# Attention tiles of 64 queries by 128 keys in place of 128 by 256

## What is computed

```python
x = x + layernorm(attention(layernorm(x)))
x = x + layernorm(ffn(layernorm(x)))

# attention: Q, K, V = x @ W.T + b, split into 16 heads
scores = Q @ K.T / sqrt(32) - (i - j)     # keys j <= query i; others -inf
out = softmax(scores) @ V                 # then @ Wo.T + bo
# ffn: x @ Hadamard, rounded per row to 4 bits, times a ternary weight
```

## Time and profile before

| | us |
|---|---|
| median of 3 runs | 1519.39 (1518.03 to 1520.32) |
| the profiled execution | 1518.89 |
| its span | 1517.2 |
| TensorE busy | 1410.3 (93%) |
| VectorE busy | 1110.3 (73%) |
| ScalarE busy | 744.7 (49%) |
| GpSimd busy | 566.5 (37%) |
| DMA queue of SP, share of 16 engines | 23.8% |

### The profile page before, as it was taken

The page is one execution under the profiler, slowest core; times in us unless marked ns, Lnnn a source line. Parts: engine busy times, 40 slices in busy tenths (PEclk is TensorE's granted clock), DMA queues, the critical chain, the costliest instruction groups (busy, mean ns, idle before and its releaser), DMA issues.

```text
span 1517.2 us, 39677 instructions
## 1 busy us (share of the span) xinstructions
PE 1410.3 (93%) x16320; PEld 954.9 (63%) x16320; DVE 1110.3 (73%) x2737; ACT 744.7 (49%) x1587; POOL 566.5 (37%) x618
## 2 busy tenths in 40 slices
PE   3789999999999999999999999999999999999852
PEld 2556666677656666666666766666666766666521
DVE  4667777777877777787777777877777787776662
ACT  3245554545545555555555545455454555554521
POOL 1132443333344443343444333344433334443321
PEclk9899999999999999999999999999999999999985
DMA  7322333222233322122333212233322222322010
GB/s 221 80 65 54 86 85 85 71 60 69 58 84 85 85 76 65 58 77 66 85 85 85 63 59 79 57 85 86 85 71 64 64 60 82 86 71 72 20 37 16
DMA packets 62073, 111.69 MB, mean 74 GB/s; under 512 B 13344, under 2 KB 14112, under 8 KB 61792
## 3 DMA queue, kind: packets, MB, share of 16 engines
q1 hardware_dynamic: 57200, 92.06, 23.8%
q0 software_dynamic: 4688, 17.04, 3.0%
HBM read 41.43 MB, written 16.78 MB: 38 GB/s over the span
## 4 chain that ended last, share of the span: by engine, by line
PE 73%; DVE 15%; ACT 4%; issue 3%; POOL 3%; DMA 1%; POOLq 0%; SPq 0%; DVEq 0%; ACTq 0%
PE f_job L977 38%; PE f_o L1100 10%; PE f_st L1081 6%; PE f_job L1131 4%; PE f_job L1149 3%; PE f_job L1006 2%; PE f_job L1123 2%; PE f_job L1049 2%; PE f_job L1061 2%; ACT f_y L505 2%; POOL f_z L377 2%; DVE f_bst L751 1%; DVE f_small L800 1%; ACT f_xTh L444 1%; PE f_job L1139 1%
## 5 line engine op out<-in xcount | busy, mean ns | idle before, releaser
L479 ACT ACTIVATE f_PT<-f_st 128x512 f32<-128x512 f32 (+1 forms) x512 | 262.9, 569 | 117.0 <-PE f_st L1081 117.0
L356 POOL TENSOR_SCALAR_AFFINE_SELECT f_PT<-f_PT 128x1024 f32<-128x1024 f32 x128 | 142.6, 1114 | 352.9 <-ACT f_PT L479 352.9
L705 DVE SCALAR_TENSOR_TENSOR f_stage<-f_job,f_bias,f_stage 128x256 f16<-128x256 f32 x256 | 112.0, 479 | 182.1 <-ACT f_stage L457 182.1
L350 POOL TENSOR_TENSOR f_small<-f_small,f_minus_half 128x2 f32<-128x2 f32 x128 | 98.3, 768 | 371.8 <-DVE f_small L684 285.8
L457 ACT ACTIVATE f_stage<-f_job,f_bias 128x256 f16<-128x256 f32 x256 | 107.5, 471 | 187.9 <-PE f_job L977 187.9
L1100 PE MATMUL f_o<-f_PT,f_V 128*32 128x128 f32 (+1 forms) x2816 | 172.3, 316 | 1.7 <-POOL f_PT L356 1.7
L1100 PE MATMUL f_o<-f_PT,f_ones 128*32 128x128 f32 (+1 forms) x2816 | 169.1, 312 | 0.0
L1081 PE MATMUL f_st<-f_stacks 128*128 128x128 f16 (+1 forms) x1408 | 150.1, 240 | 5.0 <-ACT f_PT L479 3.6
L977 PE MATMUL f_job<-f_xTh,f_wqh 128*128 128x256 f16 x512 | 140.5, 274 | 11.7 <-DVE f_wkl L603 5.9
L362 POOL TENSOR_TENSOR f_OTl<-f_o,f_OTh 128x256 f16<-128x256 f32 x128 | 84.7, 672 | 174.4 <-ACT f_OTh L493 174.4
L1081 PEld LDWEIGHTS f_st<-f_stacks 128*128 128x128 f16 x1408 | 116.5, 98 | 50.7 <-issue 7.1
(11 more groups left out here) (145 smaller groups left out, 3260.7 us busy)
## 6 DMA issues: line engine op xcount, KB each, us to landing
f_stacks<-f_stage SPq DMA_DIRECT2D x384, 128.0 KB, 2.4
f_xin<-x SPq DMA_DIRECT2D x32, 512.0 KB, 4.8
f_xres<-x SPq DMA_DIRECT2D x32, 512.0 KB, 4.1
out<-f_z POOLq DMA_DIRECT2D x32, 512.0 KB, 3.3
f_stacks<-rows_const SPq DMA_DIRECT2D x3, 512.0 KB, 5.7
f_stacks<-wqT SPq DMA_DIRECT2D x1, 1024.0 KB, 7.8
f_stacks<-wkT SPq DMA_DIRECT2D x1, 1024.0 KB, 10.5
f_stacks<-wvT SPq DMA_DIRECT2D x1, 1024.0 KB, 10.8
```

Of the source, the lines that this page charges most:

```text
L350: nc.gpsimd.tensor_tensor(dst, src, minus_half[:], ALU.pow).then_inc(done, 1)
L356: nc.gpsimd.affine_select(out=d, in_=d, compare_op=ALU.is_ge, fill=0.0, base=0, pattern=[[0, 4], [0, 2], [1, P]], channel_multiplier=-1).t ...
L479: nc.scalar.activation(PT[g % 2][:, r, lo:D], ps_st[r % 2][:, lo:D], ACT.Exp, scale=1.0 / SS).then_inc(expd, 1)
L705: nc.vector.scalar_tensor_tensor(stage[:, 2 * m + 1, g, :], bank("qk", g)[:, m * W2:(m + 1) * W2], bias[:, m, g:g + 1], stage[:, 2 * m, g, ...
```

## The change

Attention is cut by 64 queries. A tile of 64 queries now takes 128 keys: the 64 at its own place and the 64 before it. The chunks of 64 keys alternate between the upper and lower half of the partitions, so that each tile of queries has one chunk in each half and needs one product for its values. An odd chunk's two key chunks are one tile of `V`; an even chunk's lie in two tiles, so `Vmix` holds the lower half of V's tile beside the upper half of the tile before. It is filled by three on-chip DMAs a step (`mix_values`), issued by SyncE behind `restack`.

- `keys`: 5 products of 64 keys for each head (4 in the first step of a sequence) in place of 3 of 128, with 256 result columns in place of 512. Two heads share a PSUM bank and one semaphore increment.
- `exps`: one activation over two heads in place of two. In the first step of a sequence, two smaller ones.
- `clear_future`: two affine selects of half the columns, the first of them on 64 partitions.
- `weigh`: for each head four value products of 64 columns and one sum product of 256, with no accumulation; it waits for `v_mixed`, not `v_kept`.
- `V` has two buffers in place of three, `Vmix` has three, `PT` is half as large.

```diff
-        def parts(s):
-            return ([(s, 0, 0, P, 2 * P)] + ([(s - 1, 1, 0, 0, P)] if s % PER else [])
-                    + [(s, 1, 1, 3 * P, P)])
+        def keys_of(s):
+            last = [(1, s - 1, 3, 0, 1)] if s % PER else []
+            return [(0, s, 0, 0, 2)] + last + [(1, s, 1, 1, 2), (0, s, 2, 2, 2), (1, s, 3, 3, 1)]
+
+        def values_of(s, chunk):
+            keys = slice(0, P if chunk or s % PER else SUB)
+            return keys, (V[s % 2] if chunk % 2 else Vmix[s % 3])[keys, chunk // 2]
...
+            def mix_values(n):
+                sp.wait_ge(v_kept, TP * n + TP)
+                until(sp, pv_done, 4 * (n - 1))
+                lower, upper = slice(0, SUB), slice(SUB, P)
+                sp.dma_start(Vmix[n % 3][lower], V[n % 2][lower]).then_inc(v_mixed, 16)
+                sp.dma_start(Vmix[n % 3][upper, 1], V[n % 2][upper, 0]).then_inc(v_mixed, 16)
+                sp.dma_start(Vmix[(n + 1) % 3][upper, 0], V[n % 2][upper, 1]).then_inc(v_mixed, 16)
...
                 if has(s + 1):
                     restack(s + 1)
+                    mix_values(s + 1)
...
             def clear_future(s, g):
-                pool.wait_ge(expd, NH * s + 4 * g + 4)
-                d = PT[g % 2][:].rearrange("p r (a c) -> p r a c", c=P)[:, :, 1::2, :]
-                nc.gpsimd.affine_select(out=d, in_=d, compare_op=ALU.is_ge, fill=0.0, base=0,
-                                        pattern=[[0, 4], [0, 2], [1, P]],
-                                        channel_multiplier=-1).then_inc(masked, 1)
+                pool.wait_ge(expd, 2 * (4 * s + g) + 2)
+                tiles = PT[g % 2][:].rearrange("p r (t c) -> p r t c", c=P)
+                for odd in range(2):
+                    d = tiles[0:P if odd else SUB, :, :, odd * SUB:(odd + 1) * SUB]
+                    nc.gpsimd.affine_select(out=d, in_=d, compare_op=ALU.is_ge, fill=0.0, base=odd * SUB,
+                                            pattern=[[0, 4], [0, TP], [1, SUB]],
+                                            channel_multiplier=-1).then_inc(masked, 1)
...
             def keep_v(n, t):
...
                 until(act, pv_done, 4 * (n - 1))
+                until(act, v_mixed, (n - 1) * (16 * 3))
...
             def exps(s, g, half):
...
+                act.wait_ge(keyed, 2 * (4 * s + g) + half + 1)
+                until(act, pv_done, 4 * s + g - 1)
+                dst, src = PT[g % 2][:, 2 * half:2 * half + 2, :], ps_st[half][:].rearrange("p (r n) -> p r n", r=2)
+                if s % PER:
+                    nc.scalar.activation(dst, src, ACT.Exp, scale=1.0 / SS).then_inc(expd, 1)
...
             def keys(s, g, half):
...
+                until(pe, expd, 2 * (4 * s + g) + half - 1)
+                for i in range(2):
+                    h = 4 * (2 * half + i) + g
+                    for upper, js, c, q, w in keys_of(s):
+                        mm = pe.matmul(ps_st[half][upper * SUB:(upper + 1) * SUB,
+                                                   i * W2 + q * SUB:i * W2 + (q + w) * SUB],
+                                       Ks[js % 3][:, h, c * SUB:(c + 1) * SUB],
+                                       Qs[s % 3][:, h, q * SUB:(q + w) * SUB], start=True, stop=True)
+                mm.then_inc(keyed, 1)
...
             def weigh(s, g):
-                pe.wait_ge(masked, 4 * s + g + 1)
+                pe.wait_ge(masked, 2 * (4 * s + g) + 2)
...
-                    pe.wait_ge(v_kept, TP * s + TP)
+                    pe.wait_ge(v_mixed, (s + 1) * (16 * 3))
...
+                for c in range(W2 // SUB):
+                    keys, v = values_of(s, c)
+                    for r in range(4):
+                        rows = slice(r * HD, (r + 1) * HD)
+                        pe.matmul(dst[rows, c * SUB:(c + 1) * SUB], v[:, g * P + r * HD:g * P + (r + 1) * HD],
+                                  weights[keys, r, c * SUB:(c + 1) * SUB], start=True, stop=True)
+                for lo, hi in ((0, W2),) if s % PER else ((0, SUB), (SUB, W2)):
+                    keys, _ = values_of(s, lo // SUB)
+                    for r in range(4):
+                        mm = pe.matmul(dst[r * HD:(r + 1) * HD, W2 + lo:W2 + hi], ones[keys], weights[keys, r, lo:hi],
+                                       start=True, stop=True)
                 mm.then_inc(pv_done, 1)
```

41 lines of the change are left out of this document (11 added, 30 removed).

## The result

| | before | after |
|---|---|---|
| median (us) | 1519.14 (4 runs) | 1605.13 (1604.62 to 1605.91, 4 runs) |
| the profiled execution | 1518.89 | 1605.35 |
| its span | 1517.2 | 1603.5 |
| steps in the middle of the run | 43.5 to 44.1 | 46.0 to 47.9 |

The changed kernel takes 1.0566 times as long (95% interval 1.0548 to 1.0585): 86 us slower, where 30 us faster was forecast. A step is 47.0 us on average in place of 43.9. The time is outside the range and on the other side of zero.

The account below looks back on a forecast made before the run. VectorE's chain up to turn_x2 was taken to be as long as TensorE's work. Savings of 1.0 us in 24 steps with prior keys and 0.7 in 8 without made 30 us, so 1489 us, range 1460 to 1520.

Parts of the forecast that it names:

- What bounds the kernel: Up to turn_x2, VectorE's chain is as long as TensorE's work, so TensorE savings come through only as that chain shortens.
- weigh with prior keys: One weigh call on TensorE falls from 1.88 us to 1.05, saving 0.83 for each of four.
- keys amid full-width work: A keys call among full-width TensorE products costs 0.43 us against 0.44, change-over included; counted as no gain.
- rival 3: Loads of narrow weights on TensorE don't hide: weigh 1.44 us, keys 0.65, total 1513 us; chance 0.10.
- Transfers: Three more DMAs a step for values and mixing, 512 KB together, block nobody: cost 0, at most 5 us once per step.
- Behind T0: After T0, the start of turn_x2 (L1123), a step with prior keys gets 0.7 us shorter, from weigh's 0.83.
- VectorE's 1.19 idle: In steps with prior keys, VectorE's 1.19 us wait for ScalarE's inverse of weigh(s,0) goes away.
- From the end of `z_columns` to T0: Stretch of VectorE's chain before turn_x2: 11.10 us with a 0.61 wait for GpSimd's power and a 0.9 stall behind a select.
- the 25.5 us of the earlier trace: TensorE's wait at turn_x2 for VectorE's x2_norm, 9 times over the run, read as eight steps without prior and one more.
- VectorE's chain up to T0: VectorE's work before turn_x2 gets 0.3 us shorter a step; bounds 0.2 worse with both select stalls, 1.6 better with none.
- rival 4: GpSimd's selects stall VectorE longer, deciding from a pair of 1.6 us on; at 2.2 us the total is 1557; chance 0.13.
- Rival 1: VectorE's chain takes over as the bound: 1489 us, the forecast itself, own range 1470 to 1514; chance 0.70.

Follow-up runs that it names:

- e16: Changed kernel, own 64 keys always in the upper partitions, one select on 128 partitions, 16 products a keys call in place of 10: 1530.98 us, ratio 1.0081.
- e6: Changed kernel with the three transfers of mix_values left out from the fourth step on: 1603.94 us, ratio 1.0565.
- e3: Changed kernel with 12 products of 512 columns, results unread, put on TensorE ahead of turn_x2(k,0): 1547.11 us, ratio 1.0193.
- e4: Kernel before with each select of 1024 columns split in two of 512, both on 128 partitions: 1515.99 us, ratio 0.9985.
- e13: Changed kernel with the two selects in the other order, the 128-partition one first: 1604.15 us, ratio 1.0558.
- e15: Changed kernel with both selects on 128 partitions in the 24 steps with prior keys: 1542.66 us, ratio 1.0158.
- e1: Changed kernel with VectorE's square of qscale (L848) moved from behind scale_out to behind level(k-1,1): 1515.6 us, ratio 0.9982.
- e5: Kernel before with weigh cut to 512 columns, leaving out the previous tile's keys: 1527.35 us, ratio 1.0065.
- e8: e1 with weigh(s,2) moved ahead of turn_x2(k,0) in TensorE's order: 1466.86 us, ratio 0.9666.
- e2: Changed kernel with one select of 1024 columns on 128 partitions for the pair in the 24 steps with prior keys: 1535.51 us, ratio 1.0119.
- e12: e8 with keys(s,3,1) moved ahead of turn_x2(k,0) as well: 1470.0 us, ratio 0.9686.
- e9: e1 with 7 products of 512 columns without use ahead of turn_x2(k,0): 1496.7 us, ratio 0.9861.
- e11: Kernel before with the square of qscale placed later, behind the first bn_stats of z: 1518.67 us, ratio 1.0002.

## Why the prediction was wrong

**Right, and borne out.** What bounds the kernel: TensorE does wait for VectorE at `turn_x2` in nearly every step, 31 times. weigh with prior keys: 1.05 forecast, 1.01 measured. keys amid full-width work: 0.43 forecast; 0.36 to the start of the next plus 0.10 on the products behind (the 12 of `out_product` take 2.69 in place of 2.59 us) is 0.46, so indeed no gain there. Narrow loads hide (rival 3 falls, also with 16 of them in e16). Transfers: 0 (e6). Behind T0: 0.7 forecast, 0.79 in e3. VectorE's 1.19 idle is gone. From the end of `z_columns` to T0: 11.10 with both stalls forecast, 11.05 measured (734.06 to 745.11). That this fits so well is in part luck: the wait for GpSimd's `power` is there (0.61), but the stall is another, 0.81 in `residual` and none in L801, the L778 of before.

**Wrong in reading or size, without much effect.** weigh without prior is 1.43, no shorter than its 1.44, where 1.0 was forecast. keys was counted as nothing everywhere, but a narrow product follows some calls: ahead of weigh a call is 0.36 where it was 0.54, ahead of `scores` 0.25 where it was 0.54. A select of half the columns is 0.64 (e4), between the 0.55 and 0.81 of the two scalings; an undisturbed pair is 1.28, where 1.4 was taken. And the 25.5 us of the earlier trace rows are not eight steps and one more: they are seven of 1.56 us, and 5.95 and 8.64 us at the last two `turn_x2`, where the pipeline runs empty.

**The step that failed first: "VectorE's chain up to T0", a gain of 0.3 with bounds −0.2 to +1.6.** From the start of `scale_out` to T0 the chain was 17.33 us (688.09 to 705.42) and is 18.80 (726.31 to 745.11): 1.47 longer, far outside the bounds. Term by term, from one row's start to the next: L848 +1.71, `front_norm` L712 +0.42, L858 +0.44, against −1.29 for the idle and −0.32 for another small operation; then the wait for `power` ahead of `residual` and the gap around it +0.68, `residual` beside a select pair +0.81, and −0.98 for L769, which no longer meets a select (1.39 before). The prediction knew the mechanism: it wrote that VectorE's small operations stand still while a select runs, and made it rival 4. But it took its bounds from the stretch behind `z_columns`, where it had rows. From the start of `z_columns` on, the chain did get 0.32 shorter (12.36 to 12.04), as forecast; ahead of that it got 1.79 longer (4.97 to 6.76), where the sum had nothing. There stands L825, which already showed 0.74 for an operation that costs 0.15 alone. And it put rival 4's turning point at a pair of 1.6 us. Undisturbed the pair is 1.28, below it, and the two pairs of the chain at 1.70 and 1.73 are above it, so rival 4 was right in part; but the largest piece, L848's 1.71, came beside an undisturbed pair. What grew there was not the select but the stretch of GpSimd work that keeps VectorE out, from 1.1 to 3.3 us, by the squares behind it. Besides how long the select is, the question was what GpSimd runs next. The trace of before could not have given the answer: there L825 got in ahead of the squares, and only a run with a select on 64 partitions (e13, e15) shows otherwise.

What the Trainium skill says on this (GPSIMD Engine Reference, Specifications: the two engines share SBUF interfaces, with contention for VectorE instructions that have two SBUF inputs) agrees with L848, L858 and L799, which have two SBUF inputs each, being hit, and with 0.15 for the same operation in e1, where GpSimd runs nothing. `front_norm`, a `tensor_scalar` with one tensor and two columns as inputs, was hit as well: 1.41 in place of 0.99. That a select on 64 partitions changes how long VectorE waits rests on e13 and e15 alone.

**The step that was missing: the clock.** Every line of the sum was priced at full clock. In its main loop the kernel before was idle ahead of `turn_x2` only in the steps without prior keys, and kept the full clock. The change takes TensorE work out in front of a wait that doesn't move, so each saved us becomes idle: 3.2 us a step with the VectorE loss, still 1.9 to 2.7 without it in the steps with prior keys (e1). Behind 3.17 us (after) and 2.43 (e5) the granted clock dropped to 0.5 every time, behind 2.05 (e1) mostly, behind 1.84 (e5) in 7 steps of 13, behind 1.56 and 1.18 (e8) never. It is no plain threshold: behind 3.00 it stayed full in five steps of seven in e2, and in e12 it fell once behind 1.42. What else decides is open. The bill is 58 us here (e3). The Trainium skill has a related case (TensorE: Matmul & The Clock Gate, HAM oscillation: a loop in which each round's matmuls are shorter than the wait behind them drops to the idle clock in every round). The trace agrees on the drop in every round (after), though here TensorE is busy for far longer than it waits: 43.07 us of a step's 47.56. Its remedies are to restructure the loop or to make the work larger; e8 is like the first, and e3 and e9 are a poor form of the second.

**Where the forecast gain is.** With L848's stall moved away and the clock held up by useless products, TensorE's own order unchanged, the change gives 22 us (e9, 1518.4 to 1496.7), against 30 forecast. With the reordering of e8 in place of the useless products it gives 51 us (1518.2 to 1466.9); the order is then another, with `weigh(s,2)` ahead of T0, so the two gains are not of the same kernel. Rival 1 (VectorE's chain takes over) is what then holds in the steps with prior keys. What the single terms of e8's 1.6 us a step are was not taken apart further; nor was it tried to move the squares away from the selects.

## What to carry to other kernels

A saving on TensorE ahead of a wait that doesn't move need not come out as zero: it becomes idle, and idle there can cost more than was saved (9 us in e5), so a cut in TensorE's work and a reordering that puts other work into the new gap belong in one edit. Before adding or reshaping a GpSimd instruction, list the VectorE operations that can ask while it *or what is queued behind it* runs, those with two SBUF inputs above all; with a select on 64 partitions in the run, a two-column one cost 2.4 us here. A row that takes five times its usual duration in the old trace is a term of the sum, even where the change doesn't touch it.

## What the runs showed of the hardware

- A GpSimd run (select pair, then two squares) with a select on 64 of 128 partitions in it kept VectorE's 128x2 `tensor_tensor` out until the whole run had ended, 2.44 to 2.48 us, in either order (e13, e15). With all selects on 128 partitions it got in at the end of the instruction it had met: 0.28 (e4), 0.31 (e2), 0.30 (e16), 0.43 (e15), 1.02 beside a square (e11).
- The granted clock can fall to half behind as little as 1.8 to 2.1 us without TensorE work (e5, e1), in steps of 43 to 45 us in which TensorE is otherwise over 90% busy. The same length of idle doesn't always lower it: behind 1.84 us in e5 it fell in one step and not in another, and behind 3.0 us it fell in all seven steps without prior keys of the changed kernel and in two of seven in e2.
- Ten or sixteen key products with 64-column weights take the same time, 0.36 and 0.37 us from the call's start to the next product (after, e16): six more narrow weight loads into the two column halves cost nothing that shows. Amid full-width products neither is faster than six full-width products (0.44), for the products behind then take 0.10 more.
